# Flamingo layer on one core: the weights' sums of GpSimd moved inside an attention unit, and a reordered tail

## The reference, cut to what matters

```
x (8, 100, 1024), ctx (8, 361, 1024); 32 query heads, 8 key/value heads, head size 128
xn  = layernorm(x)
kv  = concat(ctx, xn)                                  # 461 rows a batch
q   = rms_norm(xn @ Wq) ; k = rms_norm(kv @ Wk) ; v = kv @ Wv
p   = softmax(q k^T / sqrt(128)) ; o = (p v) @ Wo      # Wo (4096, 1024)
x   = x + tanh(g_xattn) * o
z   = layernorm(x)
lg  = z @ router_w^T + router_b                        # 8 experts, top 2, gates that sum to 1
h   = z @ A^T (rank 16 an expert) ; hw = h * gate
out = x + tanh(g_ffn) * 0.5 * (hw @ Bm)
```

## Time and profile before

| what | value |
|---|---|
| runs | 1715.92, 1714.4, 1715.55 us; median 1715.55 |
| profiled execution | 1715.65 us, its span 1713.8 us |
| PE busy | 1665.8 us, 97% of the span |
| DVE busy | 1239.6 us, 72% |
| POOL busy | 873.9 us, 51% |
| ACT busy | 865.1 us, 50% |

### The profile page before, as it was taken

How to read it: one execution, slowest core, us unless ns; L and a number is a source line. 1 busy time by engine, 2 the same in 40 slices (tenths; PEclk the granted TensorE clock), 3 DMA queues, 4 the chain that set the end, 5 groups by cost and what they waited for, 6 DMA issues and landing times.

```text
span 1713.8 us, 26112 instructions
## 1 busy us (share of the span) xinstructions
PE 1665.8 (97%) x9120; PEld 1475.3 (86%) x9120; DVE 1239.6 (72%) x2078; ACT 865.1 (50%) x1647; POOL 873.9 (51%) x668
## 2 busy tenths in 40 slices
PE   7999999999999999999999999999999999999996
PEld 6788888678888869899999999999999889999994
DVE  7788776677777742777777777777776876557767
ACT  5445554454444432555666565665555666443321
POOL 1454444134443320766767667788786445543320
PEclk9999999999999999999999999999999999999998
DMA  5667778636666564456555554666756557676632
GB/s 196 161 181 233 235 210 241 183 108 186 162 184 154 140 239 150 138 159 191 188 156 187 182 179 160 213 217 216 232 181 215 170 205 267 212 275 229 241 116 68
DMA packets 238502, 323.86 MB, mean 189 GB/s; under 512 B 53300, under 2 KB 193396, under 8 KB 233380
## 3 DMA queue, kind: packets, MB, share of 16 engines
q1 hardware_dynamic: 237796, 315.65, 59.8%
q10 hardware_dynamic: 576, 6.55, 0.9%
HBM read 212.18 MB, written 109.97 MB: 188 GB/s over the span
## 4 chain that ended last, share of the span: by engine, by line
PE 70%; DVE 18%; issue 4%; ACT 4%; DMA 2%; POOL 0%; DVEq 0%; SPq 0%; ACTq 0%; POOLq 0%
PE bank L973 21%; PE bank L975 20%; PE bank L974 20%; DVE mx L1923 4%; PE bank L1111 3%; DVE wq_lo L1805 3%; DVE q_lo L1897 3%; PE bank L1078 2%; DVE pT_lo L1917 2%; DMA kT_d<-kst 1%; PE bank L1007 1%; ACT pr L1539 1%; DVE q_raw L1875 1%; DVE nm L1929 1%; DVE wo_lo L1943 1%
## 5 line engine op out<-in xcount | busy, mean ns | idle before, releaser
L901 POOL TENSOR_SCALAR pr<-pr,rr 100x461 f32<-100x461 f32 x256 | 370.2, 1454 | 231.6 <-DVE rr L1938 231.6
L973 PE MATMUL bank<-w_hi,a_hi 128*128 128x512 f32 (+1 forms) x856 | 340.8, 398 | 11.7 <-DVE a_lo L1713 8.6
L975 PE MATMUL bank<-w_hi,a_lo 128*128 128x512 f32 (+1 forms) x856 | 334.8, 391 | 0.0
L974 PE MATMUL bank<-w_lo,a_hi 128*128 128x512 f32 (+1 forms) x856 | 334.3, 390 | 0.0
L1539 ACT ACTIVATE pr<-bank,nm,rq 100x461 f32<-100x461 f32 x256 | 188.8, 737 | 187.6 <-DVE nm L1929 186.2
L855 POOL TENSOR_TENSOR msk<-ssk,epst 128x4 f32<-128x4 f32 (+1 forms) x60 | 23.5, 391 | 348.5 <-DVE ssk L1744 348.5
L973 PEld LDWEIGHTS bank<-w_hi,a_hi 128*128 128x128 f32 (+1 forms) x856 | 157.8, 184 | 48.8 <-issue 9.7
L1923 DVE TENSOR_REDUCE mx<-bank 100x1 f32<-100x461 f32 x256 | 160.6, 627 | 48.7 <-PE bank L975 47.2
L975 PEld LDWEIGHTS bank<-w_hi,a_lo 128*128 128x128 f32 (+1 forms) x856 | 157.5, 184 | 38.0
L973 PE MATMUL bank<-xT_hi,wq_hi 128*128 128x400 f32 x512 | 188.9, 369 | 0.5 <-issue 0.5
L974 PEld LDWEIGHTS bank<-w_lo,a_hi 128*128 128x128 f32 (+1 forms) x856 | 158.0, 185 | 34.8
(11 more groups left out here) (154 smaller groups left out, 3635.1 us busy)
## 6 DMA issues: line engine op xcount, KB each, us to landing
kT_d<-kst SPq DMA_DIRECT2D x56, 512.0 KB, 5.7
v_d<-vst SPq DMA_DIRECT2D x56, 512.0 KB
kT<-kT_d SPq DMA_DIRECT2D x64, 361.0 KB, 4.5
kvr<-ctxT SPq DMA_DIRECT2D x44, 512.0 KB, 6.2
wq_raw<-Wq SPq DMA_DIRECT2D x32, 512.0 KB, 5.8
tb<-Wo SPq DMA_DIRECT2D x16, 1024.0 KB, 8.3
wt_d<-tb SPq DMA_DIRECT2D x16, 1024.0 KB, 8.0
wo_raw<-wt_d SPq DMA_DIRECT2D x16, 1024.0 KB, 7.4
```

The lines of the kernel that those rows point to most:

```text
L901: pool.tensor_scalar(pr[0:NQ, u % 2, i], pr[0:NQ, u % 2, i], rr[0:NQ, i:i + 1], None, ALU.mult).then_inc(p_done, 1)
L973: pe.matmul(o, lh, rh, start=start, stop=False, skip_group_check=more)
L974: pe.matmul(o, lh, rl, start=False, stop=False, skip_group_check=more)
L975: return pe.matmul(o, ll, rh, start=False, stop=stop, skip_group_check=more)
```

## The change

Nothing is computed otherwise; instructions move, and four of them change the engine.

1. `WT_AT` moves each weight sum one unit later, and in a unit the sums now stand ahead of the four scales, behind a wait for the unit's first maxima (`mx_done`). The sums of unit u used to stand behind its scales.
2. `unit_rms` moves from ahead of a unit's scales (u = 3, 7, ...) to behind the scales of the unit before.
3. The early sums, one a unit from 34 to 49, take place once in two units from 19 to 49.
4. `low_rank(3)` and `route_top(3)` move inside the last half chunk; `up(3)` moves ahead of `turn_out(6)`.
5. The last four norms move from DVE to ACT, as scale and bias of one activation. POOL computes the bias, -mean * rstd, in two further small instructions.

```diff
 for _n in range(4 * WT_STEPS):
-    WT_AT.setdefault(max(-1, (_n - 4) * 6 // 7), []).append(_n)
+    WT_AT.setdefault(max(-1, (_n - 4) * 6 // 7 + 1), []).append(_n)
...
-S3_AT = 34
 S3_STEPS = GQ * TB
+S3_AT = [19 + 2 * n for n in range(S3_STEPS)]
...
-                if 0 <= u - S3_AT - 2 < S3_STEPS:
-                    store_s3(u - S3_AT - 2)
-                if 0 <= u - S3_AT < S3_STEPS:
-                    load_s3(u - S3_AT)
+                if u - 2 in S3_AT:
+                    store_s3(S3_AT.index(u - 2))
+                if u in S3_AT:
+                    load_s3(S3_AT.index(u))
...
             for u in range(UNITS):
-                if u % TB == TB - 1 and u + 1 < UNITS:
-                    unit_rms(u + 1)
+                if u in WT_AT:
+                    pool.wait_ge(mx_done, 4 * u + 1)
+                for i in WT_AT.get(u, ()):
+                    weight_sum(i)
                 for i in range(R):
                     scale(u, i)
-                for i in WT_AT.get(u, ()):
-                    weight_sum(i)
-                if 0 <= u - S3_AT - 1 < S3_STEPS:
-                    early_sum(u - S3_AT - 1)
+                if u % TB == TB - 2 and u + 2 < UNITS:
+                    unit_rms(u + 2)
+                if u - 1 in S3_AT:
+                    early_sum(S3_AT.index(u - 1))
...
+                if t >= TB:
+                    pool.tensor_scalar(mv2[0:NQ, t, 2:3], mv[0:NQ, t, 0:1], -1.0, 0.0, ALU.mult, ALU.add).then_inc(mean_done, 1)
+                    pool.wait_ge(mean_done, t - TB + 1)
+                    pool.wait_ge(rs2_done, t + 1)
+                    pool.tensor_tensor(mv2[0:NQ, t, 3:4], mv2[0:NQ, t, 2:3], mv2[0:NQ, t, 1:2], ALU.mult).then_inc(scaled_done, 1)
...
                     chunk_head(TAIL0 + n // 2, n % 2 * 2 + i)
+                    if (n, i) == (4 * GQ - 1, 0):
+                        low_rank(TB - 1)
...
-            for do, t in ((turn_out, a), (turn_out, b), (turn_h, a - 1), (turn_out, c), (turn_y, a), (up, a - 1), (low_rank, a),
-                          (turn_out, d),
+            for do, t in ((turn_out, a), (turn_out, b), (turn_h, a - 1), (up, a - 1), (turn_out, c), (turn_y, a), (low_rank, a),
+                          (turn_out, d), (turn_y, b), (low_rank, b), (turn_h, a), (turn_y, c), (up, a), (low_rank, c),
...
+            def norm(t):
+                act.wait_ge(scaled_done, t - TB + 1)
+                act.wait_ge(t2_done, t - 1)
+                act.activation(y[0:NQ, t % 2], x1[0:NQ, t % 4], ACT.Identity, bias=mv2[0:NQ, t, 3:4],
+                               scale=mv2[0:NQ, t, 1:2]).then_inc(y_done, 1)
...
-            for do, t in ((turned_y, a), (exps2, a), (turned_y, b), (turned_h, a), (turned_y, c), (exps2, b),
-                          (turned_h, b), (turned_y, d), (exps2, c), (turned_h, c), (exps2, d), (turned_h, d)):
+            for do, t in ((exps2, a - 1), (turned_h, a - 1), (norm, a), (turned_y, a), (norm, b), (exps2, a), (turned_y, b),
+                          (norm, c), (turned_h, a), (turned_y, c), (exps2, b), (norm, d), (turned_h, b), (exps2, c),
+                          (turned_y, d), (turned_h, c), (exps2, d), (turned_h, d)):
...
+            route_top(TB - 1)
             accumulators(P3)
-
             a, b, c, d = range(TB, B)
-            for do, t in ((route_top, a - 1), (residual, a), (route_gates, a - 1), (norm, a), (residual, b), (final, a - 1),
-                          (residual, c), (norm, b), (route, a),
-                          (norm, c), (residual, d), (route, b), (final, a), (norm, d), (route, c), (final, b), (route, d),
-                          (final, c), (final, d)):
+            for do, t in ((route_gates, a - 1), (residual, a), (residual, b), (final, a - 1), (residual, c), (route, a),
+                          (residual, d), (route, b), (final, a), (route, c), (final, b), (route, d), (final, c), (final, d)):
```

More of the change, by code:

```diff
@@ L199, in build @@
         mv = sb("mv", [P, B, 2])
-        mv2 = sb("mv2", [P, B, 2])
+        mv2 = sb("mv2", [P, B, 4])
         rstd = sb("rstd", [P, B, 2])
@@ L412, in build @@
         va2_done = sem("va2_done")
+        mean_done = sem("mean_done")
+        scaled_done = sem("scaled_done")
         rs2_done = sem("rs2_done")
@@ L1309, in _ @@
                     chunk_head(TAIL0 + n // 2, n % 2 * 2 + i)
+                    if (n, i) == (4 * GQ - 1, 0):
+                        low_rank(TB - 1)
                 for i, t in sorted(FFN_AT.get(n, ())):
-                    stages[i](t)
+                    if n < 4 * GQ - 1:
+                        stages[i](t)
             a, b, c, d = range(TB, B)
-            for do, t in ((turn_out, a), (turn_out, b), (turn_h, a - 1), (turn_out, c), (turn_y, a), (up, a - 1), (low_rank, a),
-                          (turn_out, d),
-                          (turn_y, b), (low_rank, b), (turn_h, a), (turn_y, c), (up, a), (low_rank, c), (turn_h, b), (up, b),
-                          (turn_y, d), (low_rank, d), (turn_h, c), (up, c), (turn_h, d), (up, d)):
+            for do, t in ((turn_out, a), (turn_out, b), (turn_h, a - 1), (up, a - 1), (turn_out, c), (turn_y, a), (low_rank, a),
+                          (turn_out, d), (turn_y, b), (low_rank, b), (turn_h, a), (turn_y, c), (up, a), (low_rank, c),
+                          (turn_h, b), (up, b), (turn_y, d), (low_rank, d), (turn_h, c), (up, c), (turn_h, d), (up, d)):
                 do(t)
@@ L1698, in _ @@
                     (chunk_heads if n % 2 else chunk_weights)(m)
-            exps2(TB - 1)
-            turned_h(TB - 1)
             a, b, c, d = range(TB, B)
-            for do, t in ((turned_y, a), (exps2, a), (turned_y, b), (turned_h, a), (turned_y, c), (exps2, b),
-                          (turned_h, b), (turned_y, d), (exps2, c), (turned_h, c), (exps2, d), (turned_h, d)):
+            for do, t in ((exps2, a - 1), (turned_h, a - 1), (norm, a), (turned_y, a), (norm, b), (exps2, a), (turned_y, b),
+                          (norm, c), (turned_h, a), (turned_y, c), (exps2, b), (norm, d), (turned_h, b), (exps2, c),
+                          (turned_y, d), (turned_h, c), (exps2, d), (turned_h, d)):
                 do(t)
```

## The result

The changed kernel takes 1742.4 us (median of 1742.09, 1742.22, 1748.07 and 1742.52) against 1715.0 of the kernel before, run beside it: a ratio of 1.0168, 95% interval [1.0146, 1.0190]. The forecast was 1724.4 in a range of 1697 to 1731: the side was right, the loss is three times what was forecast, and the time lies outside the range. The profiled execution took 1742.09, its span 1740.3.

What follows compares the result with a forecast made beforehand. PE, busy in nearly the whole span, was taken as the bound. Units +11.8 and tail -3.0 gave +8.8 on 1715.65, so 1724.5, or 1724.4 as median; own range 1717 to 1731, with rival (a) 1697 to 1731.

Steps and rivals of the forecast that it cites:

- The bound and the gain of wq_lo: Attention units: PE's own work is 11.35 us; wq_lo falls to 1.23, which alone would gain 14.9 us over 50 units.
- The tie and its price: Behind the first maxima, POOL's sum starts 0.05 ahead of nm, holding it about 1.06 us; 37 units take 11.99 each.
- In units 3, 7 ... 51, 13 of the 50, nm is free: 11.36.: Units with unit_rms ahead of the sum: nm starts before unit_rms ends, so it isn't held; 11.36 us each, 147.7 together.
- the units' term: Units 2 to 51: 594.7 us against 582.88 before, so +11.8 us.
- The slack of 0.42: In a unit, how long nm can be held before the hold costs time, one for one from there: 0.42 us.
- rival (c): Attention units: the hold on nm lasts as long as the sum, 16 us more, 1740 in all; chance 0.04.
- Crowded units: Early sums from unit 23 on cost 2 us, double sums with late scales in units 31 and 43 cost 1.4.
- The tail: Behind the last output chunk: moved low_rank(3), route_top(3), up(3) and norms gain 3.0 us, range -6 to +1.
- accumulators to end: In the tail, the stretch from DVE's accumulators to the end gets 4.85 us shorter.
- (a): Attention units: nm wins the tie against the sum, units take 11.36 us, the kernel 1700.4; chance 0.28.
- 37 x 0.43 = 16: Extra cost in 37 units if nm is held for the sum's whole 1.49 us: 16 us more, 1740.
- The 12.4: Upper bound in us for a unit where nm is held for the sum's whole 1.49: 11.99 + 0.43.

Runs made afterwards that it cites:

- sum_behind_nm: The changed kernel, but each weight sum waits for nm(u,0) instead of the unit's first maxima: 1703.4 us, ratio 0.9927 to the kernel before.
- four_waits: The changed kernel, but the wait for the first maxima ahead of each weight sum is written four times: 1704.7 us, ratio 0.9927 to the kernel before.
- nm_gate_after_rms: The changed kernel, but in units 3, 7 ... 51 alone the weight sum waits for nm(u,0): 1728.0 us, ratio 1.0066 to the kernel before.
- sum_released_early: The changed kernel, but in units 3, 7 ... 51 the weight sum has no wait for the maxima: 1727.4 us, ratio 1.0061 to the kernel before.
- tail_only: The kernel before with only the change's tail (low_rank(3), norms, orders of the tail): 1714.1 us, ratio 0.9980 to the kernel before.
- two and four waits: The changed kernel with the wait for the first maxima ahead of each weight sum written twice or four times: 1705.2 us and 1704.7 us.

## Why the prediction was wrong

**The bound and the gain of wq_lo: right.** wq_lo takes 1.23, the first maxima start 1.01 to 1.03 behind every unit's start, and where nm is free a unit takes 11.34 to 11.39 (sum_behind_nm); I had 11.36.

**The tie and its price: right.** I had nm held for 1.06 and units of 11.99. Measured are 1.26 - 0.16 = 1.10 and, over the 37 units, 610.91 - 166.51 = 444.4, where I had 443.6. That the tie is the cause is shown by four_waits, which only lets the sum go 0.17 later: its 37 units take 421.4.

**The failed step: "In units 3, 7 ... 51, 13 of the 50, nm is free: 11.36."** I reasoned from POOL's execution: unit_rms ends after nm has started, so the sum can't be first. That order came out (the sum starts 0.63 behind nm), but it didn't free nm. What counted was when the sum was released, and by the 0.05 of the other units its wait on the maxima ended ahead of nm there, too. nm was held through the rest of unit_rms and the sum behind it (1.9), in units 7 and 31 through one instruction more (3.14, 2.95), and in the other units from 23 on to the end of the early sum (1.64 to 1.73). The 13 units took 166.5, not the 147.7 + 2 + 1.4 = 151.1 of my sum: 15.4 of the 16.2 that the units' term was short. The slack of 0.42 that I gave for rival (c) fits these units well: (1.92 - 0.16) - 0.42 = 1.34 against 12.68 - 11.36 = 1.32, and (3.14 - 0.16) - 0.42 = 2.56 against 2.57 in unit 7. So the size follows from the hold alone; the hold was what I had set to nothing there. nm_gate_after_rms and sum_released_early take it away and give 13 to 14 us back. The step had no bound of its own in the range: I bounded the hold of the 37 units from both sides, and the 13 with a single number. What remains open is why a release 2 us ahead, or that of unit 11 with four waits, doesn't hold nm.

**Crowded units.** Early sums and double sums were to cost 3.4 by late scales. In sum_behind_nm, where they are all that is left, units 2 to 51 take 575.1 against 50 x 11.36 = 568.0, so they cost 7; that price was hidden in the holds here. The eight units with an early sum cost 4.0 of it. I had counted a second sum in units 31 and 43 only and passed over those in 7, 13, 19, 25, 37 and 49, which cost 3.3.

**The tail: right in sum, partly by luck.** Forecast -3.0, measured -3.3 from unit 56 on; "accumulators to end" 4.85 shorter, measured 5.39. final(3) has no idle ahead, y stands on ACT. A norm on ACT takes 1.24, where I took 1.0; up is worth more and the norms less than I had (3.4 and 2.3, against 1.63 and 3.2). PE's clock was granted at 0.89 and 0.68 in the eight us that hold low_rank(4), which took 3.22, where low_rank(5) took 3.95 at 0.58 before. In five of the eight kernels with this tail low_rank(4) took 2.10, and in tail_only, one of them, up(3) took 2.01 and 1.86 for its two halves instead of the 1.10 and 1.02 here: where the low clock falls differs from profile to profile.

**The rest.** 1.7 of the spans' difference lies before unit 2. The kernels whose code is the same up to there reached unit 2 at 709.59 (before) and 711.86 (tail_only), so this is the spread of executions and not the change.

**The rivals.** (a) would have been the outcome with a few hundredths more on POOL's queue: 1700.4 forecast, 1704 to 1705 measured with two and four waits. I gave it 0.28, fair for a lead of 0.05. (c), the slower end at 1740, came near the time by luck. Its mechanism is what the trace shows: the hold lasts as long as the sum, nm ends at 739.04 and the sum at 739.03. But it adds nothing in the 37 units, because the sum takes 1.30 there. The 1.49 that I put in is a sum in its old place, beside wq_lo; the 58 sums of units 2 to 51 now take 1.285 in the mean. So 37 x 0.43 = 16 was wrong, and the 15.4 of the 13 units stood in its place. The Trainium skill ("SBUF — State Buffer", "Who interferes with whom") has the shared pair held for the whole instruction. nm behind a sum agrees with it here, 739.04 against 739.03, while nm behind a scale of 1.44 was held for 0.43. The 12.4 that the prediction drew from it took the whole 1.49 as the hold. A sum of 1.30 that starts 0.05 ahead of nm holds it for 1.26 - 0.16 = 1.10; less the slack of 0.42 that is 0.68 on top of 11.36, so 12.04, and the 37 units are 12.0.

## What to carry to other kernels

Two engines that wait for one event can start within hundredths of a microsecond of each other (0.05 here); if their instructions exclude each other, that order decides, and if the small one is on the critical path, let the large one wait for the small one's result, not for the common event. When reading who comes first, take the moment at which the wait ends, not the moment at which the trace shows execution: an instruction let go behind a long one may already bar the other engine (nm took 1.92 in unit 3), though not in every case (unit 11 with four waits). Give every class of a repeated step its own two bounds; the class called free is where a forecast is lost.

## What the hardware showed beyond that

A POOL instruction of 2.9 us on 100x16 (unit_rms) doesn't hold up nm while it runs (0.16 in its midst, also with another instruction ready behind it), but a 128x512 sum let go 0.05 ahead of nm holds it to the sum's end, even though the sum begins 0.63 behind nm's start. The same sum let go 2 us ahead doesn't. Why the early release loses its hold stays open. So does how many instructions nm waits for: from unit 23 on, but for unit 31, it was let through at the end of the early sum with the weight sum next, in unit 31 behind the early sum and one weight sum, in unit 7 only behind both sums, in unit 19, also with two, behind the first. No run here moved the release in steps between 0.05 and 2 us; only unit 11, above, has leads between them, by its late nm.

A satisfied wait costs POOL's queue about 0.05 us: the sum's start behind nm's went from -0.05 with one wait to 0.00 with two and 0.12 with four.

In all of these kernels two of DVE's norms of 100x1024 take 4.28 to 4.30 instead of 0.80, as at 1640.57 of the changed kernel. There four POOL sums of 128x400 run from 1640.27 for 4.03, and the other norms on DVE have no such sums beside them. No run moved the two apart.
